# Row maxima twelve slots ahead of the scores in place of sixteen, with shifts in two equal halves, in a fused two-layer kernel

## The chip, the cores and the metric

The kernel runs as one program on one core of a Trainium2 chip. Its time is the device time of an execution in microseconds; the median of three runs before the change is 3403.16 us (3401.01 to 3411.55). TensorE does matrix products, VectorE and ScalarE work on tiles, GpSimd on a few more and on indirect transfers, and SyncE (SP) issues most of the transfers, in the order of its queue.

## The reference

Two layers over x of 16 batches x 512 positions x 128 features. Each layer normalises x and adds an "attention" and a "feed forward" part to it.

- Layer 0, first part: a small memory network is trained over chunks of the sequence and then read with queries made from every position.
- Layer 0, second part: a convolution over three positions, an attention of 16 heads of 8 features, layer normalisation, and eight experts of which all are computed and weighted by a softmax gate, then normalisation again.
- Layer 1, first part: a causal attention, a convolution of its result which gives new queries, a second causal attention with the same keys and values, and an output product.
- Layer 1, second part: 32 experts of which each position takes 8; every expert has a capacity of 128 rows.

```python
scores = jnp.einsum('bhqd,bhkd->bhqk', q, k) / jnp.sqrt(jnp.float32(dh))
attn = jax.nn.softmax(scores, axis=-1)
ctx = jnp.einsum('bhqk,bhkd->bhqd', attn, v)
...
ctx = _causal_attn(q, k, v)
...
q2 = conv_out.transpose(0, 2, 1).reshape(b, s, NUM_HEADS, HEAD_DIM)
ctx2 = _causal_attn(q2, k, v)
```

## The kernel before, in words

The program has four stages: the memory network's training (0 to about 353 us of the span), layer 0's attention (names with c_, to 1131), layer 0's experts (names with a_, to 2205), and layer 1 (names with b_, with the routed experts, r_, in between).

Both attentions use one class, `Attention`. A *turn* p is the attention of one batch: 16 in layer 0, 32 in layer 1, where each batch has a first and a second attention. In layer 1 the turns go: two firsts, then a first and a second by turns, then the last two seconds. A turn has 16 *slots* s, four *groups* g of heads with four tiles t of 128 positions each (s = 4 g + t). For a slot the kernel does three things, at different times:

1. maxima: TensorE makes the scores with the queries on the partitions (`tensor_maxima`, L1295, and the causal mask, L1301), and VectorE takes the maximum of each row (L1504). They go through a ring of two double banks, m.
2. scores: TensorE makes them again with the keys on the partitions (L1327, mask L1334), where the shift by the row maximum comes in as two extra rows of the queries' tile; ScalarE takes the exponential (L1445). They go through a ring of three banks, s.
3. values: the exponentials times the values, with the row sums (L1358). After two groups ScalarE copies the result out (`scalar_context`, L1452).

The shift rows must be in the queries' tile before the scores use them. When all maxima of some groups are there, TensorE transposes them (`tensor_shift`, L1308), VectorE negates and splits them into two bf16 rows (L1512, L1513), and SP sends them into the tile (`sync_shift`, L1273). Shift 0 covers three groups and is made in slot 12 of the turn before; shift 1 covers the fourth and is made in slot 0 of the turn itself, and is first used in slot 12.

The maxima of turn p + 1 are made in turn p, slot for slot: they run 16 slots ahead. So there is one turn at the start, p = -1, in which maxima run alone, and the last turn has scores alone.

The order is written out by hand for each engine, in loops over turns and slots; no scheduler moves anything. `extra` functions put further jobs into given slots: in layer 0 the convolution of batch p + 2 in slots 0 and 2 (L1761), its query projection in 4 (L1766), keys in 5 (L1769), values in 6 (L1776), and in the last turn the first batch of the next stage, by the table `FIRST`: z (the gate's and the memory's input), x1, gate, query, hidden, memory (L1787 to L1813). There VectorE makes the gate's probabilities in the query job, after an exponential on ScalarE, and GpSimd then does sixteen operations, two for each expert (L1742, L1743); VectorE's last work is the chain of the memory job, to L1927. The next stage starts with a barrier. In layer 1 the projections of a first attention are in slots 0, 4 and 8 (L2958, L2962, L2979), the convolution for a second in 7 and 9 (L2968), the normalising of a context in 6 (L1265), the output product in 10 (L2987), and the routed experts in turns 0 to 8 by the table in `Routed`: LOCAL, SELECT (the rows of four experts are found; five VectorE operations, L2725 to L2731), ROWS, UP (two products, L2645), GATE (VectorE, L2737, L2738), HIDDEN (transposes, L2651), DOWN (L2656 and scaling on ScalarE, L2702).

SP's queue in a turn of layer 1 is: store the spread sums and context of the former turn's second half, shift 1, the experts' weights, a read of the sum, the reciprocals' store and the reads of scale and context (`sync_inverse`: three waits), then the first half's spread, the twelve row transfers of turn p + 2 (`sync_rows`, each 16 partitions by 8 heads), and shift 0 of turn p + 1.

## Time and profile before

| | |
|---|---|
| median of three runs | 3403.16 us |
| the profiled execution | 3429.25 us, its span 3427.3 us |
| TensorE matmul busy | 3143.2 us, 92% of the span |
| VectorE, ScalarE, GpSimd busy | 2539.8 (74%), 2058.4 (60%), 851.4 (25%) us |
| granted TensorE clock, mean | 0.967 |
| layer 0's maxima on VectorE (L1504) | 512 x 1.212 us |
| layer 1's maxima on VectorE (L1504) | 768 x 1.041 us |

The page cuts the span in 40 slices and gives each engine's busy share in tenths; a matmul counts as busy while it is in the pipeline, so a full TensorE row means that it is never without work and not that it runs at its peak. A line of the timeline has the start in us, the time of the merged instructions in us, the engine, the line of the kernel, what is written from what, the shapes, the count, and in brackets the idle time before it and what ended that.

### The profile page before, as it was taken

The numbers are of one execution on the slowest core, as the hardware profiler recorded it, in microseconds if no ns is written. First come the engines' busy times: TensorE is split into PE (matmuls) and PEld (weight loads), VectorE is DVE, ScalarE is ACT, GpSimd is POOL, SyncE is SP. The second block draws the span as 40 slices with busy tenths as digits, with TensorE's granted clock in tenths as the row PEclk, the third lists the DMA queues.
The fourth block names the chain that finished last, engine by engine and source line by source line (L and its number), as shares of the span: only waits on it lengthen the run. The fifth ranks groups of instructions, "written<-read, shape, count | busy, mean of one in ns | idle before, by whom it ended". The sixth has DMA issues, their size and how long they took to land. (4 is left out here: it accounts for less than half of the span.)

```text
span 3427.3 us, 83140 instructions
## 1 busy us (share of the span) xinstructions
PE 3143.2 (92%) x33099; PEld 1864.5 (54%) x33099; DVE 2539.8 (74%) x5024; ACT 2058.4 (60%) x4153; POOL 851.4 (25%) x772
## 2 busy tenths in 40 slices
PE   6887599999999999999999999688999999999997
PEld 6876222222222677777777777545555555555553
DVE  5876788888887376677667667677777887777874
ACT  6774188888888444343443434146667766776775
POOL 3321111111111332332242233213333211111110
PEclk9998699999999999999999999789999999999998
DMA  4100222222221101011010001223333233222222
GB/s 144 32 13 1 57 74 83 83 80 81 77 71 61 37 28 31 22 33 35 22 33 29 29 23 33 54 75 89 87 87 79 85 94 86 76 82 82 80 64 62
DMA packets 234970, 204.86 MB, mean 60 GB/s; under 512 B 74340, under 2 KB 190852, under 8 KB 234500
## 3 DMA queue, kind: packets, MB, share of 16 engines
q1 hardware_dynamic: 227620, 194.71, 19.7%
q0 software_dynamic: 6144, 4.72, 1.0%
q8 instruction: 224, 3.67, 0.5%
q10 hardware_dynamic: 864, 0.79, 0.1%
q14 instruction: 118, 0.97, 0.1%
HBM read 73.61 MB, written 59.39 MB: 39 GB/s over the span
## 5 line engine op out<-in xcount | busy, mean ns | idle before, releaser
L1504 DVE TENSOR_REDUCE b_maxima<-psum 128x2 f32<-128x1024 f32 (+3 forms) x768 | 780.0, 1041 | 256.8 <-PE psum L1301 226.3
L1445 ACT ACTIVATE b_prob<-psum 128x512 f32<-128x512 f32 (+2 forms) x1536 | 725.8, 526 | 323.4 <-PE psum L1334 297.8
L1504 DVE TENSOR_REDUCE c_maxima<-psum 128x2 f32<-128x1024 f32 x512 | 592.2, 1212 | 60.4 <-PE psum L1295 59.6
L1445 ACT ACTIVATE c_prob<-psum 128x512 f32<-128x512 f32 x1024 | 547.4, 600 | 113.5 <-PE psum L1327 96.9
L2268 PEld LDWEIGHTS psum<-consts_layer,a_hid 128*128 128x128 f32 x4096 | 476.2, 192 | 53.6 <-issue 53.3
L2268 PE MATMUL psum<-consts_layer,a_hid 128*128 128x128 f32 x4096 | 477.8, 274 | 0.0
L2258 PE MATMUL psum<-a_x1t,consts_layer 128*128 128x512 f32 x1024 | 461.9, 595 | 14.1 <-ACT a_hid L2328 7.6
L2328 ACT ACTIVATE a_hid<-psum,consts_layer 128x512 f32<-128x512 f32 x512 | 347.1, 687 | 196.4 <-PE psum L2258 189.7
L1358 PE MATMUL psum<-b_prob,b_v 128*32 128x128 f32 (+3 forms) x5632 | 405.5, 374 | 15.1 <-ACT b_c L1452 14.0
L1327 PE MATMUL psum<-b_qa,b_ka 64*128 64x512 bf16 (+3 forms) x2048 | 349.0, 305 | 45.8 <-ACT b_prob L1445 30.4
L2495 DVE SCALAR_TENSOR_TENSOR a_acc<-psum,a_gprob,a_acc 128x128 f32<-128x128 f32 x512 | 143.7, 342 | 262.4 <-PE psum L2268 246.8
L1295 PE MATMUL psum<-b_ka,b_qa 62*128 62x512 bf16 (+3 forms) x2048 | 306.1, 306 | 28.6 <-DVE b_maxima L1504 17.3
L1358 PE MATMUL psum<-c_prob,c_v 128*32 128x256 f32 (+1 forms) x3840 | 320.2, 405 | 1.7 <-ACT c_prob L1445 0.6
L2258 PEld LDWEIGHTS psum<-a_x1t,consts_layer 128*128 128x128 f32 x1024 | 187.3, 191 | 217.1 <-issue 196.9
L1327 PEld LDWEIGHTS psum<-b_qa,b_ka 64*128 64x128 bf16 x2048 | 123.3, 94 | 304.3 <-ACT b_prob L1445 209.6
L1334 PE MATMUL psum<-b_kmask,b_pick 64*128 64x64 bf16 x4096 | 245.0, 191 | 0.5 <-issue 0.5
L1295 PE MATMUL psum<-c_ka,c_qa 62*128 62x512 bf16 x1024 | 209.9, 389 | 31.3 <-DVE c_maxima L1504 17.3
L1327 PE MATMUL psum<-c_qa,c_ka 64*128 64x512 bf16 x1024 | 218.3, 387 | 19.1 <-ACT c_prob L1445 18.7
L1301 PEld LDWEIGHTS psum<-b_qmask,b_pick 64*128 64x128 bf16 x4096 | 201.4, 97 | 53.6 <-issue 8.0
L1301 PE MATMUL psum<-b_qmask,b_pick 64*128 64x64 bf16 x4096 | 228.4, 191 | 1.6 <-issue 1.5
L1334 PEld LDWEIGHTS psum<-b_kmask,b_pick 64*128 64x128 bf16 x4096 | 187.1, 95 | 46.4 <-issue 4.2
L1358 PEld LDWEIGHTS psum<-c_prob,c_v 128*32 128x32 f32 x3840 | 75.6, 108 | 204.3 <-issue 111.6
(398 smaller groups left out, 4203.6 us busy)
## 6 DMA issues: line engine op xcount, KB each, us to landing
b_qa<-b_part SPq DMA_DIRECT2D x192, 128.0 KB
b_context<-b_c SPq DMA_DIRECT2D x64, 256.0 KB, 2.1
c_qa<-c_part SPq DMA_DIRECT2D x96, 128.0 KB, 2.5
b_ka<-b_part SPq DMA_DIRECT2D x96, 128.0 KB
c_ka<-c_part SPq DMA_DIRECT2D x90, 128.0 KB, 2.5
c_context<-c_c SPq DMA_DIRECT2D x32, 256.0 KB, 2.1
b_scale<-b_inverse SPq DMA_DIRECT2D x64, 128.0 KB
b_unscaled<-b_context SPq DMA_DIRECT2D x64, 128.0 KB
```

The lines of the kernel that those rows point to most:

```text
L1295: last = nc.tensor.matmul(out[:, half, k0:k0 + w], qa[rows, hh, t * P:(t + 1) * P], ka[rows, hh, 0:w], start=True, stop=not self.causal)
L1301: last = nc.tensor.matmul(out[:, half, k1:k1 + HALF], self.pick[n][rows, :], self.qmask[rows, :], start=False, stop=n == 1)
L1327: last = nc.tensor.matmul(outs[half][:, k0:k0 + w], ka[rows, hh, t * P:(t + 1) * P], qa[rows, hh, q0:S], start=True, stop=not self.causal)
L1334: last = nc.tensor.matmul(outs[half][:, k0 + n * HALF:k0 + (n + 1) * HALF], self.pick[n][rows, :], self.kmask[rows, :], start=False, stop= ...
L1358: product = nc.tensor.matmul(self.acc[32 * j:32 * (j + 1), q0:q1], self.values(p)[:, t, column:column + 32], self.prob[:, s % 2, j, q0:q1] ...
L1445: self.nc.scalar.activation(out, src, ACT.Exp, scale=SCALE).then_inc(self.s.free, 1)
L1504: self.nc.vector.reduce_max(out, src, X).then_inc(self.m.free, 1)
L2258: nc.tensor.matmul(bank[4 + u % 3], K("up0", e * F0 + f * P, P), x1t[n][:, :], start=True, stop=True).then_inc(up_ready.sem, 1)
L2268: last = nc.tensor.matmul(tiled(2 + e % 2)[:, t, :], hid[:, e % 2, f, t * P:(t + 1) * P], K("down0", (e * FC + f) * D, D), start=f == 0, s ...
L2328: nc.scalar.activation(hid[:, e % 2, f, :], bank[4 + u % 3], ACT.Relu, bias=K("upb0", u, 1)).then_inc(hid_ready.sem, 1)
L2495: last = nc.vector.scalar_tensor_tensor(acc[n][:, t, :], tiled(2 + e % 2)[:, t, :], gprob[n][:, t, e:e + 1], acc[n][:, t, :], ALU.mult, AL ...
```

## The change

- Maxima run 12 slots ahead (`LEAD`): in slot s of turn p the maxima of turn p + 1, slot s - 4, and in the first four slots those of turn p, slots 12 to 15 (`leading`).
- Shift 0 and shift 1 cover two groups each. Shift 0 stays in slot 12 of the turn before; shift 1 is made in slot 4 (before: slot 0) and first used in slot 8 (before: slot 12).
- SP sends shift 1 after `sync_inverse` of the former turn's second half, no longer before the weights.
- In layer 0's last turn the first batch's jobs stand in slots 4, 8, 9, 10, 11, 13 in place of 2, 6, 7, 8, 10, 13.
- The routed jobs: SELECT 5 for 4, UP 6 and 7 for 5 and 6, GATE 10 for 7, HIDDEN 11 for 9, DOWN 13 for 11.

```diff
--- before.py
+++ after.py
@@ -169,7 +169,8 @@
 BUFFERS = 3
 SPREAD = 16
 PAIRS = G // 2
-EARLY = G - 1
+EARLY = G // 2
+LEAD = SLOTS - T
 GAP = 16
 
 
@@ -1113,8 +1114,12 @@
 
     def moved(self, p, s):
 
-        jobs = [(p, 1)] if s == 0 else [(p + 1, 0)] if s == EARLY * T else []
+        jobs = [(p, 1)] if s == SLOTS - LEAD else [(p + 1, 0)] if s == EARLY * T + SLOTS - LEAD else []
         return [job for job in jobs if self.has(job[0])]
+
+    def leading(self, p, s):
+
+        return divmod(p * SLOTS + s + LEAD, SLOTS)
 
     def inverting(self, p, s):
 
@@ -1143,7 +1148,7 @@
                     for j in self.heads(s, 0):
                         self.s.add("exp", p, s, j)
                 jobs = [("shift", *job) for job in self.moved(p, s)] + more_m(p, s)
-                maxima = [("max", p + 1, s, u) for u in self.units(s)] if self.has(p + 1) else []
+                maxima = [("max", *self.leading(p, s), u) for u in self.units(s)] if self.has(self.leading(p, s)[0]) else []
                 for job in maxima[0:1] + jobs + maxima[1:]:
                     self.m.add(*job)
                 for job in more_s(p, s):
@@ -1369,8 +1374,9 @@
                     self.tensor_scores(pe, p, s, u)
 
             def maxima(u):
-                if self.has(p + 1) and u in self.units(s):
-                    self.tensor_maxima(pe, p + 1, s, u)
+                q, r = self.leading(p, s)
+                if self.has(q) and u in self.units(r):
+                    self.tensor_maxima(pe, q, r, u)
 
             def values(slots, half=None):
                 q, r = divmod(p * SLOTS + s - slots, SLOTS)
@@ -1491,10 +1497,8 @@
         if self.causal:
             t = T - 1 - t
         w = (t + 1) * P if self.causal else S
-        if g < EARLY:
-            out = self.maxima[0][:, :].rearrange("p (f g u t) -> p f g u t", f=2, g=EARLY, u=2)[:, :, g]
-        else:
-            out = self.maxima[1][:, :].rearrange("p (f u t) -> p f u t", f=2, u=2)
+        n, g = divmod(g, EARLY)
+        out = self.maxima[n][:, :].rearrange("p (f g u t) -> p f g u t", f=2, g=EARLY, u=2)[:, :, g]
         src = self.m.bank("max", p, s, u)
         if self.together(s):
             out, src = out[:, :, :, t], src[:, :, 0:2 * w].rearrange("p f (u k) -> p f u k", u=2)
@@ -1528,9 +1532,10 @@
 
     def vector_turn(self, dve, p, own, extra):
         for s in range(SLOTS):
-            units = self.units(s) if self.has(p + 1) else ()
+            q, r = self.leading(p, s)
+            units = self.units(r) if self.has(q) else ()
             for u in units[0:1]:
-                self.vector_maxima(dve, p + 1, s, u)
+                self.vector_maxima(dve, q, r, u)
             for job in self.moved(p, s):
                 self.vector_shift(dve, *job, own)
             for job in self.inverting(p, s):
@@ -1538,7 +1543,7 @@
                     self.vector_inverse(dve, *job)
             extra(p, s)
             for u in units[1:]:
-                self.vector_maxima(dve, p + 1, s, u)
+                self.vector_maxima(dve, q, r, u)
 
 
 @dataclass
@@ -1629,7 +1634,7 @@
         att.late(ctx, kept)
         CONVOLVE, QUERIES, KEYS, VALUES = (0, 2), 4, 5, 6
         LAST = NB - 1
-        FIRST = {2: "z", 6: "x1", 7: "gate", 8: "query", 10: "hidden", 13: "memory"}
+        FIRST = {4: "z", 8: "x1", 9: "gate", 10: "query", 11: "hidden", 13: "memory"}
 
         def job_of(p, s):
 
@@ -1677,8 +1682,6 @@
                 load_x(0)
                 load_x(1)
                 for p in range(-2, NB):
-                    if att.has(p):
-                        att.sync_shift(sp, p, 1)
                     if att.has(p - 1):
                         att.sync_spread(sp, p - 1, PAIRS - 1)
                     if att.has(p + 2):
@@ -1688,6 +1691,9 @@
                         load_x(p + 4)
                     if att.has(p - 1):
                         att.sync_inverse(sp, p - 1, PAIRS - 1)
+                    if att.has(p):
+                        att.sync_shift(sp, p, 1)
+                    if att.has(p - 1):
                         sp.wait_ge(att.normalised, p)
                         sp.dma_start(ctxt_d[(p - 1) * P:p * P, :], ctxt[:, :]).then_inc(ctxt_stored, 16)
                     if att.has(p):
@@ -2532,7 +2538,7 @@
 
 
 
-    LOCAL, SELECT, ROWS, UP, GATE, HIDDEN, DOWN = 2, 4, 1, (5, 6), 7, 9, 11
+    LOCAL, SELECT, ROWS, UP, GATE, HIDDEN, DOWN = 2, 5, 1, (6, 7), 10, 11, 13
     TOTAL, BEFORE, INCLUDED = 9, 10, 11
 
     def __init__(self, ctx, csem, nc, K, att, start, chosen, gate_up, down, table_d, sum_d):
@@ -2886,8 +2892,6 @@
                 for p in range(-1, len(turns) + 1):
                     if att.has(p - 1):
                         att.sync_spread(sp, p - 1, PAIRS - 1)
-                    if att.has(p):
-                        att.sync_shift(sp, p, 1)
                     routed.sync_weights(sp, p)
                     if p in outputs:
                         i, b = order.index(p), outputs[p].batch
@@ -2902,6 +2906,7 @@
                     if att.has(p - 1):
                         att.sync_inverse(sp, p - 1, PAIRS - 1)
                     if att.has(p):
+                        att.sync_shift(sp, p, 1)
                         att.sync_spread(sp, p, 0)
                     if att.has(p + 2):
                         att.sync_rows(sp, p + 2)
```

TensorE at the start of layer 0's attention, turn -1 and the end of the turn before: c_ka and c_qa are keys and queries (L1295, maxima), c_xt the convolution's input (L1761), c_xc its result (L1766 queries, L1769 keys, L1776 values). Before:

```order
L1776 MATMUL psum<-consts_layer,c_xc 128x128 x4
L1295 MATMUL psum<-c_ka,c_qa 128x512 x2
L1761 MATMUL psum<-c_xt,consts_layer 128x256 x3
L1295 MATMUL psum<-c_ka,c_qa 128x512 x8
L1761 MATMUL psum<-c_xt,consts_layer 128x256 x3
L1295 MATMUL psum<-c_ka,c_qa 128x512 x8
L1766 MATMUL psum<-c_xc,consts_layer 128x512
L1295 MATMUL psum<-c_ka,c_qa 128x512 x4
L1769 MATMUL psum<-c_xc,consts_layer 128x512
L1295 MATMUL psum<-c_ka,c_qa 128x512 x4
```

And in the changed kernel, whose lines are numbered up to six higher:

```order
L1782 MATMUL psum<-consts_layer,c_xc 128x128 x4
L1767 MATMUL psum<-c_xt,consts_layer 128x256 x6
L1300 MATMUL psum<-c_ka,c_qa 128x512 x2
L1772 MATMUL psum<-c_xc,consts_layer 128x512
L1300 MATMUL psum<-c_ka,c_qa 128x512 x4
L1775 MATMUL psum<-c_xc,consts_layer 128x512
L1300 MATMUL psum<-c_ka,c_qa 128x512 x4
L1782 MATMUL psum<-consts_layer,c_xc 128x128 x4
```

The two convolutions of slots 0 and 2 stand ahead of the first maxima now, and the query projection behind the first pair of them; eight pairs of maxima fewer stand ahead of the keys' projection.

SP in a turn of the middle of layer 1: b_spread and b_context are the stores of the row sums and the context, b_before a read of the sum, b_inverse, b_scale and b_unscaled the steps of `sync_inverse`, b_shift1 shift 1. Before:

```order
L1245 DMA b_spread1<-b_c1 128x1x32
L1246 DMA b_context<-b_c1 128x512
L1273 DMA b_qa0<-b_shift1 2x8x128 x2
L2900 DMA b_before<-sum 128x4x128
L1253 DMA b_inverse<-b_spread1 128x32
L1257 DMA b_scale<-b_inverse 64x1x512
L1260 DMA b_unscaled<-b_context 64x1x512
L1245 DMA b_spread0<-b_c0 128x1x32
L1246 DMA b_context<-b_c0 128x512
```

Changed:

```order
L1250 DMA b_spread1<-b_c1 128x1x32
L1251 DMA b_context<-b_c1 128x512
L2904 DMA b_before<-sum 128x4x128
L1258 DMA b_inverse<-b_spread1 128x32
L1262 DMA b_scale<-b_inverse 64x1x512
L1265 DMA b_unscaled<-b_context 64x1x512
L1278 DMA b_qa0<-b_shift1 2x16x128 x2
L1250 DMA b_spread0<-b_c0 128x1x32
L1251 DMA b_context<-b_c0 128x512
```

Shift 1 has moved from the third place to behind the context's read, with 16 head rows in place of 8.

VectorE in turn 2 of layer 1, from slot 4 on: r_tiles to r_index is the selection, b_cpad the normalising, r_th and r_h the gate, a row of b_maxima one reduction. Before:

```order
L1504 TENSOR_REDUCE b_maxima<-psum 128x2
L2725 TENSOR_SCALAR r_tiles<-psum 128x4
L2726 TENSOR_SCALAR r_below<-psum,consts_layer 128x512
L2729 TENSOR_REDUCE r_slot<-r_below 128x4
L2730 TENSOR_TENSOR r_slot<-r_tiles,r_slot 128x4
L2731 TENSOR_SCALAR r_index<-r_slot,consts_layer 128x4
L1504 TENSOR_REDUCE b_maxima<-psum 128x2 x3
L1504 TENSOR_REDUCE b_maxima<-psum 128x2x2
L1265 TENSOR_TENSOR b_cpad<-b_unscaled,b_scale 128x512
L1504 TENSOR_REDUCE b_maxima<-psum 128x2x2
L2737 SCALAR_TENSOR_TENSOR r_th<-r_th,r_gu 128x384
L2738 TENSOR_TENSOR r_h<-r_th,r_gu 128x384
```

Changed:

```order
L1508 TENSOR_REDUCE b_maxima<-psum 128x2
L1516 TENSOR_SCALAR b_shift<-psum 32x128
L1517 SCALAR_TENSOR_TENSOR b_shift<-psum,b_shift 32x128
L1508 TENSOR_REDUCE b_maxima<-psum 128x2 x2
L2731 TENSOR_SCALAR r_tiles<-psum 128x4
L2732 TENSOR_SCALAR r_below<-psum,consts_layer 128x512
L2735 TENSOR_REDUCE r_slot<-r_below 128x4
L2736 TENSOR_TENSOR r_slot<-r_tiles,r_slot 128x4
L2737 TENSOR_SCALAR r_index<-r_slot,consts_layer 128x4
L1508 TENSOR_REDUCE b_maxima<-psum 128x2
L1508 TENSOR_REDUCE b_maxima<-psum 128x2x2
L1270 TENSOR_TENSOR b_cpad<-b_unscaled,b_scale 128x512
```

The selection has moved behind the maxima of slot 4 and the first of slot 5, shift 1 stands ahead of it, and the gate is gone from here (it follows in slot 10).

## Rows read from the trace of the kernel before

**Rows 1.** Windows: stretch in us, busy us by engine with counts, clock, DMA, GB/s
```profile
391.00:421.00 30.00, 18.40 (x66) 4.59 (x64) 28.88 (x28) 2.12 (x4) 6.32 (x4) 0.62 0.20 55
478.00:1029.00 551.00, 533.22 (x4918) 158.10 (x4916) 486.74 (x485) 465.64 (x874) 98.30 (x65) 1.00 0.27 79
1029.00:1067.00 38.00, 36.27 (x366) 9.06 (x366) 37.36 (x39) 34.41 (x66) 1.27 (x1) 1.00 0.22 66
1124.00:1136.00 12.00, 5.58 (x23) 2.41 (x16) 5.82 (x12) 1.97 (x3) 3.18 (x5) 0.72 0.33 98
2205.00:2237.00 32.00, 24.19 (x236) 14.46 (x238) 23.59 (x27) 1.76 (x4) 13.03 (x19) 0.61 0.31 76
2650.00:3341.00 691.00, 644.06 (x11570) 355.83 (x11572) 549.91 (x641) 489.48 (x1041) 116.90 (x96) 1.00 0.29 81
3346.00:3378.00 32.00, 30.10 (x584) 16.45 (x576) 27.09 (x33) 23.63 (x51) 1.27 (x1) 1.00 0.16 50
3378.00:3410.00 32.00, 27.65 (x353) 12.06 (x349) 2.74 (x7) 22.17 (x48) 1.28 (x1) 0.84 0.22 66
```

**Rows 2.** Timeline, start of layer 0's attention, TensorE
```profile
378.07 0.61 PE L1295 MATMUL psum<-c_ka,c_qa 62*128 62x512 bf16 x2 [13.52 <-DMA c_ka<-c_part]
378.61 2.93 PE L1761 MATMUL psum<-c_xt,consts_layer 128*128 128x256 f32 x6
...
391.02 2.00 PE L1766 MATMUL psum<-c_xc,consts_layer 128*128 128x512 f32 x2
```

**Rows 3.** Timeline, last turn of layer 0's attention, all engines
```profile
1089.73 6.38 ACT L1445 ACTIVATE c_prob<-psum 128x512 f32<-128x512 f32 x12
...
1094.44 0.16 DVE L120 SCALAR_TENSOR_TENSOR c_tmp<-c_rstd 128x4 f32<-128x4 f32 x1
...
1101.59 0.66 PE L1804 MATMUL psum<-consts_shared,a_q 128*128 128x128 f32 x4
...
1106.95 1.05 POOL L1742 TENSOR_TENSOR c_share<-a_gprob,consts_layer 128x512 f32<-128x512 f32 x1 [0.19 <-DVE a_gprob L1910]
...
1115.98 2.05 PE L1813 MATMUL psum<-memw1t,c_ht 128*128 128x128 f32 x16
...
1121.00 1.12 DVE L120 SCALAR_TENSOR_TENSOR c_tmp<-c_rstd 128x4 f32<-128x4 f32 x1
...
1125.80 1.26 POOL L1743 TENSOR_TENSOR a_acc<-a_acc,c_share 128x512 f32<-128x512 f32 x1
...
1129.02 0.69 DVE L1927 TENSOR_TENSOR a_q<-a_q,c_rest 128x512 f32<-128x512 f32 x1
...
1131.28 9.07 PE L2258 MATMUL psum<-a_x1t,consts_layer 128*128 128x512 f32 x16 [6.42 <-PEq L1671]
```

**Rows 4.** Timeline, start of layer 1, TensorE
```profile
2205.26 0.61 PE L1295 MATMUL psum<-b_ka,b_qa 62*128 62x512 bf16 x2 [7.39 <-POOL b_cpad L2929]
...
2213.60 2.07 PE L2962 MATMUL psum<-b_xt,consts_layer 128*128 128x512 f32 x2
```

**Rows 5.** Timeline, shifts and scores in turns 0, 1 and 10 of layer 1
```profile
2281.07 1.13 SPq L1273 DMA_DIRECT2D b_qa<-b_shift  x2
...
2283.87 0.61 PE L1327 MATMUL psum<-b_qa,b_ka 64*128 64x512 bf16 x2 [4.56 <-DMA b_qa<-b_shift]
...
2667.74 0.60 SPq L1260 DMA_DIRECT2D b_unscaled<-b_context  x1
...
2672.59 0.39 PE L1327 MATMUL psum<-b_qa,b_ka 64*128 64x512 bf16 x2
```

**Rows 6.** Waits (us in all, times, longest) of 2237 to 2590 us; then timeline, turn 0
```profile
PE psum L1295 <- DVE b_maxima L1504: 9.7, 13, 2.9
PE psum L1327 <- DMA b_qa<-b_shift: 7.4, 2, 4.6
...
2251.88 2.04 DVE L2730 TENSOR_TENSOR r_slot<-r_tiles,r_slot 128x4 f32<-128x4 f32 x1
...
2256.21 0.34 PE L1295 MATMUL psum<-b_ka,b_qa 62*128 62x384 bf16 x2 [2.88 <-DVE b_maxima L1504]
```

## The prediction

> **What bounds the kernel now.** I read the summary and the slices of the page first: TensorE is busy for 92% of the span, and its slices fall at the start of each stage and at the very end. So I cut the span where both attentions start and stop [rows 1]. In the middle of layer 0's attention TensorE is busy for 533.2 of 551 us and VectorE for 486.7: TensorE decides. In the stretch from 1029 to 1067, which has no projections left, VectorE is busy for 37.4 of 38 us: without projections the maxima decide, two reductions of 1.21 us in a slot, 2.4 us. In the middle of layer 1 TensorE has 644 of 691 us. A change of order that moves no work off TensorE can win nothing there; it can only win where TensorE idles, and that is at the ends. At the first slots of layer 0's attention only maxima run, at half clock (0.62 granted), TensorE 18.4 of 30 us busy, VectorE 28.9. The start of layer 1 looks the same (0.61, 24.2 of 32). In the last turn of layer 1 the reader is to see that taking the maxima away saves nothing: 32 us with them, 32 without, with the granted clock falling from 1.00 to 0.84.
>
> **The start of layer 0's attention.** Now the maxima of slot 0 are the first to wait for the row transfers (13.52 us of idle TensorE), and the two convolutions of the next batch, in slots 0 and 2, stand behind them; so does the query projection of slot 4, at 391.02 [rows 2]. In the changed order both convolutions stand ahead of the first maxima, inside that wait of 13.5 us: the first takes 2.93 us, the second as much, and both are hidden. Right behind the first pair of maxima comes the query projection, at the place of the convolution that now starts at 378.61. So everything from that projection on comes 391.02 - 378.61 = 12.4 us earlier. Not all of it stays: between that point and the first score VectorE's maxima set the pace, but with the key and value projections at half clock TensorE takes part in it. The query projection took 2.00 us at half clock; those of keys and values, which ran partly at full clock, have as many columns. I charge 2.0 us (bounds: 0 if the clock rises as it does now, 3.0 if all three slots wait for TensorE). Term: -10.4.
>
> **The end of layer 0's attention.** The last turn gets four slots of maxima. A slot with them takes 2.4 us, one without 6.38/3 = 2.13 us, by twelve exponentials (three slots) in 6.38 us [rows 3]: 4 x 0.28 = 1.1 us. The first batch's jobs keep their number of matmuls. The router's chain is pushed more than the rest: its query job stands at slot 10 in place of 8, while the memory job stays at 13. GpSimd starts its sixteen operations when VectorE has made the gate's probabilities, and they last from 1106.95 to 1125.80 + 1.26 = 1127.06. VectorE ends its chain at 1129.02 + 0.69 = 1129.71, and the next stage begins at 1131.28, 1.57 us later. Two slots later less what the hidden job now does behind it (it moves from 10 to 11): from the query job at 1101.59 to the memory job at 1115.98 there are 14.4 us now; afterwards there are three slots (6.4), the query matmuls (0.66), the hidden ones (two products as wide as the query projection, at full clock: about 2) and about 0.5 of waits, 9.5. So the query job, and with it GpSimd's end, comes 4.9 + 1.1 = 6.0 us later, at 1133.1, and GpSimd takes VectorE's place as the one who ends last: 1133.1 - 1129.71 = +3.4. I take 3.3 (bounds: 1.1 if ScalarE gives the exponentials as much sooner as it idles there, 5 if the sixteen stretch). Nothing hides it: the next stage starts when all engines have ended. Half clock follows TensorE's idle time there now (0.72 granted and 5.6 us busy over 1124 to 1136, rows 1); with 3 us more of it I add 1.0 (0 to 3.4).
> GpSimd and VectorE disturb each other here: the same small operation L120 takes 0.16 us at 1094.44, without GpSimd, and 1.12 at 1121.00, beside it [rows 3]. The Trainium skill, page "SBUF — State Buffer", section "SBUF: two separate sides", has a rule for it: the two share a pair of ports under an exclusive lock, and a VectorE operation with two inputs in SBUF waits for a GpSimd operation that reads SBUF. By that rule the last additions of VectorE's chain (L1925, L1927), which are free of GpSimd today, would each wait up to 1 us, VectorE would end with GpSimd, and the sum would be about 1 us higher.
>
> **The start of layer 1.** The query projection (slot 0) no longer waits for maxima; it starts at 2205.3, takes 2.07, and the maxima of slot 4 with the key projection behind them start at 2207.3 and 2208.0. Now the latter starts at 2213.60 [rows 4]. Term: -5.6 (bounds -4 and -6.5). GpSimd clears the values buffers before it makes turn 1's parts and may start those later than the projection allows, but they are wanted four slots later than before.
>
> **The end of layer 1.** Four more slots have maxima, twelve have none. A turn costs 32 us either way [rows 1]. Term: +0.5 (-1 to +2).
>
> **Shift 1.** Its transpose, two VectorE operations and two transfers move from slot 0 to slot 4, with 32 rows in place of 16 (and 32 in place of 48 for shift 0; the widths read by TensorE and VectorE are 128 either way). TensorE must have it at slot 8, before at slot 12. On SP's queue it now stands behind the reciprocal's store, the scale and the context read. In a late turn of layer 1 the last of these is issued at 2667.74 and done issuing at 2668.34; the two shift issues take 1.13, to 2669.5. From the end of issue to the release of TensorE it took 1.67 us where it was waited for (2281.07 + 1.13 to 2283.87): landing at 2671.1. Slot 8's scores start at 2672.59 [rows 5]: 1.4 us to spare. The last two turns of layer 1 have no projections and take 32 us in place of 35; slot 8 comes sooner there, and I expect a short wait in each, together +0.5 (0 to 3). In layer 0 a turn is 44 us long and the slack is larger. I found no wait for rows in the middle, so their later need wins nothing.
>
> **The eight routed turns.** Waits of TensorE here: 7.4 us in 2 for shift 0, which the change leaves at slot 12 and behind the same twelve row transfers, and 9.7 us in 13 for VectorE's maxima, most of it behind the selection [rows 6]. In turns that prepare a first attention the selection is stretched by GpSimd's parts (2.04 us for an operation on 128x4 elements) and TensorE then idles for up to 2.9 us. At slot 5 it still lies within those parts (they run 6.5 us from slot 4's key projection), so the wait moves with it; then come normalising at slot 6 and, before, the gate at slot 7. The gate's 1.1 us leave this crowded stretch and shift 1's 0.56 enter it: -0.5 in four turns, -2. But the gate at slot 10 is followed by its transposes at slot 11, not two slots later. From the end of slot 10's maxima TensorE has values, scores and maxima of slot 11 to do, 1.6 us; VectorE needs 1.23 for the maxima and 1.11 for the gate, 2.4 with the start: TensorE waits 0.8, in the turns with an output product (1.1 us more for TensorE, 0.7 for VectorE) 0.4. Eight turns: +4.8. Term: +2.8, bounds -6 (the waits behind the selection vanish) and +9 (a whole microsecond more in each). I take the reckoned one, near the middle.
>
> **Sum.** -10.4 + 3.3 + 1.0 - 5.6 + 0.5 + 0.5 + 2.8 = -7.9 us. The profiled execution took 3429.25 us (span 3427.3, 1.95 around it), 0.8% over the median of 3403.16; the terms are waits and engine times that both executions have. 3429.25 - 7.9 = 3421.3 for a profiled one, 3403.16 - 7.9 = 3395.3 for the median.
>
> **Rivals.**
> A. The routed turns gain and layer 0's end costs only the maxima: -10.4 + 1.1 - 5.6 - 2 + 0.5 = -16.4, 3387. For it: ScalarE, which gives GpSimd's chain its exponentials, is not full in a slot without maxima; TensorE's longest waits for VectorE sit at the place that is thinned. Against it: GpSimd's chain is 20 us of its own work.
> B. The start is won and spent again: the maxima-only stretch is a full half-clock stretch already, and the waits in turns 0 to 8 for transfers and GpSimd (shift 0's 4.56 us in turn 0, rows 5) fall where they fell. With 3 us lost at layer 0's start, 5 at its end and 6 in the routed turns the sum is -12.4 + 3 + 5 + 1.0 - 5.6 + 0.5 + 0.5 + 6 = -2: 3401. Against it: the worst ends must come together.
> C. Slower: shift 1 lands after slot 8 begins, in every turn of layer 1. The point is 1.4 us of slack in rows 5; the reciprocal waits for a spread's landing and two round trips to memory lie between. If the queue is 2.4 us later than reckoned, 31 turns lose 1.0 us each: -7.9 + 31 = +23, 3426. For it: shift 0, with an equal lead, is waited for in two routed turns and in some late ones; against it: shift 0 stands behind twelve row transfers, shift 1 behind three.
>
> **How the numbers follow.** This kernel's timing can tell about 0.3%, 10 us, from no change: faster is below 3393, slower above 3413. The forecast (3395, own range 3389 to 3401) has 0.55, A 0.18, B 0.14, C 0.10, the rest 0.03. Faster: 0.4 of the forecast, all of A, a little of B: 0.42. Slower: C and most of the rest, with some for a new wait that I did not see: 0.13. Same: 0.45. The range takes A in at one side and B with half of the way to C's threshold at the other: 3383 to 3410.
>
> **What would show it.** The convolutions L1767 before 378 in the idle wait, and layer 0's first score at about 409 in place of 419.6; GpSimd's last operation before the next stage, ending after VectorE's; layer 1's first maxima right behind a projection; the turns in the middle of both attentions as long as before; no wait of L1332 for b_shift at slot 8 over 0.5 us; TensorE waiting for r_h before L2657. Wrong if layer 0's first score comes later than 412, or if the steady turns change their length by more than 0.2 us: then 46 turns outweigh both ends.

## The result, and the profile after

| | us |
|---|---|
| kernel before, median of 18 runs | 3400.86 (3395.38 to 3411.55) |
| changed kernel, median of 18 runs | 3395.92 (3392.42 to 3401.26) |
| ratio, 95% interval | 0.9986 (0.9979 to 0.9992) |
| second series of the changed kernel | 3397.07 against 3399.95, 0.9984 (0.9974 to 0.9995) |
| profiled execution of the changed kernel | 3401.26, span 3399.2 |

The gain is 0.14%, 4.9 us, inside "no change" as the prediction bounds it, though it is clear of zero. The time forecast, 3395.3, is met; the movement forecast, -7.9, is 3 us too large.

The two profiles shown first can't be subtracted: 3427.3 and 3399.2 us of span are 28 us apart where the medians are 5 apart. The kernel before took about 3400 us in three of the four series and 3426.95 (17 runs) in one, which ran on another chip than the two behind it; the profile ahead of the prediction is like that one's, the changed kernel's like the others'. A third profile of the kernel before, from a series in which it took 3400 (3398.55 us, span 3396.6), is what I compare with. Both kernels are cut at the same places: first maxima, first score and last turn of layer 0, the mixture's first and last product, first score of layer 1, its turn 9, its turn 31, the end. Columns as in [rows 1]; the kernel before first:

```profile
380.60:420.90 40.30, 24.98 (x89) 8.23 (x91) 35.88 (x34) 2.32 (x4) 6.32 (x4) 0.67 0.19 53
420.90:1079.20 658.30, 636.57 (x5872) 187.59 (x5868) 584.89 (x585) 556.48 (x1045) 105.87 (x70) 1.00 0.26 77
1079.20:1132.40 53.20, 43.03 (x385) 16.73 (x382) 26.15 (x76) 36.42 (x71) 23.43 (x21) 0.96 0.14 44
1132.40:2180.90 1048.50, 1040.71 (x6204) 776.38 (x6205) 700.12 (x2630) 422.11 (x649) 335.52 (x301) 1.00 0.10 31
2180.90:2237.70 56.80, 28.44 (x263) 18.01 (x263) 38.14 (x92) 2.66 (x6) 15.11 (x21) 0.61 0.23 59
2237.70:2598.80 361.10, 334.28 (x5486) 193.22 (x5484) 286.83 (x367) 252.54 (x555) 132.76 (x136) 0.97 0.37 89
2598.80:3350.90 752.10, 702.03 (x12707) 388.74 (x12704) 601.06 (x703) 536.59 (x1142) 125.58 (x105) 1.00 0.28 80
3350.90:3396.60 45.70, 27.35 (x397) 13.61 (x393) 4.55 (x10) 24.05 (x52) 2.54 (x2) 0.87 0.24 71
```

And the changed kernel (its second profile, 3393.32 us):

```profile
377.90:407.10 29.20, 17.61 (x63) 4.46 (x63) 26.82 (x26) 1.37 (x2) 6.32 (x4) 0.62 0.22 61
407.10:1065.80 658.70, 636.99 (x5874) 188.08 (x5872) 584.73 (x585) 556.36 (x1045) 105.85 (x70) 1.00 0.26 77
1065.80:1121.80 56.00, 43.51 (x402) 16.64 (x398) 39.50 (x85) 36.60 (x71) 23.98 (x21) 0.94 0.13 42
1121.80:2170.70 1048.90, 1041.31 (x6204) 776.79 (x6205) 700.06 (x2630) 421.86 (x649) 335.34 (x301) 1.00 0.10 31
2170.70:2222.00 51.30, 24.73 (x215) 15.88 (x215) 32.12 (x86) 2.66 (x6) 14.99 (x21) 0.60 0.28 68
2222.00:2591.00 369.00, 334.19 (x5486) 193.95 (x5483) 286.79 (x367) 252.41 (x555) 129.94 (x134) 0.97 0.36 87
2591.00:3345.10 754.10, 703.45 (x12710) 389.76 (x12708) 604.93 (x703) 536.54 (x1142) 126.25 (x107) 1.00 0.28 79
3345.10:3391.40 46.30, 28.64 (x445) 14.91 (x441) 10.59 (x16) 24.00 (x51) 2.54 (x2) 0.86 0.24 70
```

In the sixth row TensorE is busy for as long in both kernels, 334 us, and the stretch is 7.9 us longer: pure waiting. One execution of a stretch varies by a few us, so each is averaged over two or three profiles that have it unchanged (for the routed turns only from series in which the kernel before took 3400 us):

| stretch | before | changed | difference | predicted |
|---|---|---|---|---|
| start of layer 0 | 41.5, 42.1, 40.3 | 29.9, 29.2, 29.9 | -11.6 | -10.4 |
| turns 0 to 14 | 658.5, 658.7, 658.3 | 658.4, 658.7, 658.2 | 0 | 0 |
| last turn, to the next stage | 53.2, 53.2, 53.2 | 57.5, 56.0, 57.6 | +3.8 | +4.3 |
| mixture of experts | 1048.9, 1048.7, 1048.5 | 1049.7, 1048.9, 1049.4 | +0.6 | 0 |
| start of layer 1 | 56.9, 57.1, 56.8 | 51.4, 51.3, 51.4 | -5.6 | -5.6 |
| turns 0 to 8, routed | 361.1, 358.1 | 368.4, 369.0, 365.3 | +8.0 | +2.8 |
| turns 9 to 30 | 756.2, 752.8, 752.2 | 756.2, 754.1, 754.4 | +1.2 | +0.5 |
| last turn and end | 49.3, 45.5, 45.7 | 47.2, 46.3, 45.8 | -0.4 | +0.5 |

The sum is -4.0, the medians' difference -4.9; the part ahead of the first maxima, 378 to 381 us in all six profiles, is not in the table. (358.1 is a kernel whose layer 1 is the kernel before's, 365.3 one whose layer 1 is the changed kernel's; both are below.) The last two rows are within the spread: four more profiles with the changed kernel's turns 9 to 30 have 752.6 to 755.6 there, and 46.3 to 49.0 in the last turn and end.

The start of layer 0, TensorE, changed kernel, first profile; it answers to [rows 2]:

```profile
366.77 2.76 PE L1767 MATMUL psum<-c_xt,consts_layer 128*128 128x256 f32 x12
380.55 0.61 PE L1300 MATMUL psum<-c_ka,c_qa 62*128 62x512 bf16 x2 [11.02 <-DMA c_ka<-c_part]
381.08 2.07 PE L1772 MATMUL psum<-c_xc,consts_layer 128*128 128x512 f32 x2
```

The convolutions L1767 now stand ahead of the wait for the row transfers, inside it. The query projection follows the first maxima by 0.53 us; before it was 391.02 - 378.07 = 12.95 [rows 2]: 12.4 us sooner, as reckoned. The start of layer 1 answers to [rows 4]; the query projection stands ahead of the first maxima, the key projection right behind them:

```profile
2201.04 2.07 PE L2963 MATMUL psum<-b_xt,consts_layer 128*128 128x512 f32 x2 [7.25 <-POOL b_cpad L2934]
2203.05 0.61 PE L1300 MATMUL psum<-b_ka,b_qa 62*128 62x512 bf16 x2
...
2203.69 2.08 PE L2967 MATMUL psum<-b_xt,consts_layer 128*128 128x512 f32 x2
```

The last turn of layer 0, all engines, answers to [rows 3]; the next stage begins at 1126.33, in its last line:

```profile
1099.67 0.96 PE L1810 MATMUL psum<-consts_shared,a_q 128*128 128x128 f32 x4
...
1103.97 1.05 POOL L1748 TENSOR_TENSOR c_share<-a_gprob,consts_layer 128x512 f32<-128x512 f32 x1 [12.74 <-DVE a_gprob L1916]
...
1120.44 4.16 DVE L1929 SCALAR_TENSOR_TENSOR c_qk<-c_qk,c_rstd,mem 128x128 f32<-128x128 f32 x4
...
1122.93 1.26 POOL L1749 TENSOR_TENSOR a_acc<-a_acc,c_share 128x512 f32<-128x512 f32 x1
...
1125.36 0.69 DVE L1933 TENSOR_TENSOR a_q<-a_q,c_rest 128x512 f32<-128x512 f32 x1
1126.33 0.23 POOL L2349 MEMSET a_zeros<- 128x160 f32 x1 [2.14 <-POOLq L1676]
```

GpSimd ends at 1124.19 and VectorE at 1126.05: VectorE is the last. Its four scalings L1929 take 4.16 us beside GpSimd; the same four took 1.14 us before, behind GpSimd's end (at 1127.12, L1923).

Before, VectorE was not the last, though the prediction reads it so: it ended at 1129.71, and SyncE, which clears the stage's 64 semaphores behind its last two stores, at 1130.8. SyncE's row of these clears, first and last start in us, kernel before, changed kernel and the run exp_early below:

```profile
L75 SPq EVENT_SEMAPHORE_RANGE_CLEAR  x64: 25/30/49, 1126.7 to 1130.8; - x64
L75 SPq EVENT_SEMAPHORE_RANGE_CLEAR  x64: 25/30/49, 1120.4 to 1124.4; - x64
L75 SPq EVENT_SEMAPHORE_RANGE_CLEAR  x64: 25/30/49, 1118.0 to 1122.1; - x64
```

The routed turns, changed kernel: TensorE's waits from 2227.4 to 2595.8 (us in all, times, longest), which answer to [rows 6], and the new wait in turn 7:

```profile
PE psum L1300 <- DVE b_maxima L1508: 8.2, 8, 2.5
PE psum L2657 <- DVE r_h L2744: 6.7, 5, 1.4
...
PE psum L1332 <- DMA b_qa<-b_shift: 6.0, 2, 4.9
...
PE psum L2657 <- ACT b_prob L1451: 1.9, 3, 0.6
```
```profile
2546.71 0.82 DVE L2743 SCALAR_TENSOR_TENSOR r_th<-r_th,r_gu 128x384 f32<-128x384 f32 x1
2547.57 0.56 DVE L2744 TENSOR_TENSOR r_h<-r_th,r_gu 128x384 f32<-128x384 f32 x1
...
2548.27 0.61 PE L2657 MATMUL psum<-consts_shared,r_h 128*96 128x128 f32 x4 [1.39 <-DVE r_h L2744]
```

The transposes of the gate's values wait in all eight turns, 6.7 + 1.9 = 8.6 us. Before they never did.

Shift 1 in turn 10 of layer 1, which answers to [rows 5]: issued until 2642.1, scores of slot 8 at 2645.9, no wait.

```profile
2640.98 1.13 SPq L1278 DMA_DIRECT2D b_qa<-b_shift  x2
...
2645.91 0.39 PE L1332 MATMUL psum<-b_qa,b_ka 64*128 64x512 bf16 x2
```

### The profile page after: what moved, and what is told of

Same layout as the page of the kernel before. It is cut to its first block and busy times, and to the rows that moved or that the text cites. A ratio compares the mean times of both kernels' runs of the same rounds, so it can differ in the third digit from the quotient of the medians.

```text
span 3399.2 us, 83140 instructions
## 1 busy us (share of the span) xinstructions
PE 3119.3 (92%) x33099; PEld 1853.6 (55%) x33099; DVE 2545.7 (75%) x5024; ACT 2058.5 (61%) x4153; POOL 851.1 (25%) x772
## 5 line engine op out<-in xcount | busy, mean ns | idle before, releaser
L1508 DVE TENSOR_REDUCE c_maxima<-psum 128x2 f32<-128x1024 f32 x512 | 592.5, 1212 | 65.3 <-PE psum L1300 64.4
L2274 PEld LDWEIGHTS psum<-consts_layer,a_hid 128*128 128x128 f32 x4096 | 476.2, 192 | 53.6 <-issue 53.3
L1300 PE MATMUL psum<-c_ka,c_qa 62*128 62x512 bf16 x1024 | 209.2, 387 | 25.7 <-DVE c_maxima L1508 14.1
L1339 PEld LDWEIGHTS psum<-b_kmask,b_pick 64*128 64x128 bf16 x4096 | 185.8, 95 | 45.7 <-issue 3.1
```

What stands on the lines that cost most here:

```text
L1300: last = nc.tensor.matmul(out[:, half, k0:k0 + w], qa[rows, hh, t * P:(t + 1) * P], ka[rows, hh, 0:w], start=True, stop=not self.causal)
L1339: last = nc.tensor.matmul(outs[half][:, k0 + n * HALF:k0 + (n + 1) * HALF], self.pick[n][rows, :], self.kmask[rows, :], start=False, stop= ...
L1508: self.nc.vector.reduce_max(out, src, X).then_inc(self.m.free, 1)
L2274: last = nc.tensor.matmul(tiled(2 + e % 2)[:, t, :], hid[:, e % 2, f, t * P:(t + 1) * P], K("down0", (e * FC + f) * D, D), start=f == 0, s ...
```

## The experiments

All were timed beside the kernel before, whose median was 3426.95 in the first series (before_again, halves16, lead_l0, slots_back), 3399.95 in the second (halves16_oldsp, after_again, gate9, exp_early) and 3400.21 in the third (before_third, l0_only, best, best_first). In names: the "routed slots" are those of the selection, up, gate, hidden and down products. The diffs are cut to the lines that matter; a plus or minus is against the kernel that the text names, the changed kernel where it names none.

**The kernel before, profiled again.** No edit.

> The kernel before, unchanged, profiled a second time. Its first profiled execution took 3429.25 us, the median of 18 is 3400.9. Theory: that execution had more half clock than most in the eight routed turns, so the second one takes 3401 +- 6 us, and the stretch from the first score of turn 0 of layer 1 to that of turn 9, 384.7 us in the first, is 363 to 370 us. Rival: the first profile is typical there, the stretch is 385 us again, and the new slots of the routed work are what shortened it to 368.4 us in the changed kernel.

3423.05 us, routed turns 381.7. The theory failed, and the rival's 385 nearly came, but not for the rival's reason: in this series all 17 runs of the kernel before took 3421 us or more. What follows is that the first profile was no odd execution, and that a profile must be compared with one from a series in which the same kernel takes the same time.

> The kernel before, unchanged, once more. Both profiles of it that there are come from where it takes 3421 to 3429 us. Theory: where it takes 3400 the routed turns (first score of turn 0 to that of turn 9 of layer 1) take 357 us (355 to 360), 26 us less, and all other stretches the same; so the changed kernel's 368.7 there are 11 to 12 us more, which is what the ends win less what is measured. Rival: the routed turns take 368 us there too, and the missing gain went elsewhere.

3398.55 us, routed turns 361.1 (expected 355 to 360, rival 368), all other stretches as in the first two profiles within a few us. The theory holds nearly: 21 to 24 us of the difference between the profiles lie in the routed turns, and on equal ground the changed kernel spends 8 us more there, not 11 to 12.

**The halves alone, lead of 16.** SP's new order stays; the first batch and the routed work have their old slots. Against the kernel before:
```diff
-EARLY = G - 1
+EARLY = G // 2
+LEAD = SLOTS
```


> Only the equal halves of the shifts and SP's new order: the maxima keep their lead of 16, and the first batch and the routed work their slots. Shift 0 is made at slot 8 and needed at slot 16. Theory: the two waits of TensorE for shift 0 in the routed turns (4.56 and 2.80 us before) vanish, nothing else moves: 4 us faster than before (0 to 7). Rival: the halves are the change's main gain: 8 us or more. Rival: shift 1 with twice the rows is late at slot 4 somewhere: slower than before by 3 us or more.

3463.26, ratio 1.0105 (1.0090 to 1.0119): 36 us slower, the last rival's direction and far more than any of the expectations. The two waits for shift 0 that were to vanish are still there (4.9 and 0.3 us here, 5.1 and 2.2 in the next run, at the start of turns 1 and 3), though its maxima are ready four slots sooner. In layer 0's last turn, all engines, shift 1 is made at slot 0, but in the new order of SP's queue it stands behind the reciprocal of slot 3 and TensorE waits 3 us for it:

```profile
1101.77 1.13 SPq L1278 DMA_DIRECT2D c_qa<-c_shift  x2
1104.81 0.40 PE L1332 MATMUL psum<-c_qa,c_ka 64*128 64x512 bf16 x2 [3.00 <-DMA c_qa<-c_shift]
```

**The same with SP's queue in its old order.** Against halves16, layer 0's loop; the same is done in layer 1's, and the later place is taken out in both:
```diff
+                    if att.has(p):
+                        att.sync_shift(sp, p, 1)
                     if att.has(p - 1):
                         att.sync_spread(sp, p - 1, PAIRS - 1)
```


> The kernel before with the shifts in equal halves alone: lead 16, and SP's queue in its old order, shift 1 ahead of the spread, the inverse and the scale. Theory: halves16 loses 36 us for two reasons, the shift jobs of slot 8 beside the values there, about 32 us in layer 1, and SP's order, 3 us in layer 0's last turn (the wait for shift 1 at its slot 8); so this one loses 30 to 33 us to the kernel before. Rival: SP's order is what costs (shift 1 behind the inverse of slot 3): this one is within 5 us of the kernel before.

3424.17, 1.0066 (1.0053 to 1.0079): 22.5 us slower by the ratio, 24.2 by the medians, where 30 to 33 were expected and 5 by the rival; layer 0's end is back at 53.3. Both of the theory's causes are there. How much each costs is not shown: halves16 lost 36 us in a series in which the kernel before took 3427, this one 22.5 in one with 3400. The waits of TensorE in layer 1 (2240 to 3410) show the larger cause:

```profile
PE psum L2977 <- DVE b_maxima L1502: 15.2, 14, 1.9
...
PE psum L1308 <- DVE b_maxima L1502: 12.6, 10, 1.9
```

The shift's transpose (L1308) waits for maxima 12.6 us, and is not among the waits of the kernel before (third profile), while the values projection (L2977) waits 15.2 (10.1 before). All of these waits are in slot 8: with a lead of 16 the equal halves put a shift job there, beside the values projection. A lead of 12 puts it on slots 4 and 12. So the halves cost with the long lead; what they are worth with the short one was not tried apart from it.

**The lead of 12 in layer 0 alone, halves in both.** The routed work has its old slots:
```diff
+    def lead(self):
+        return SLOTS if self.causal else LEAD
```


> As halves16, with the lead of 12 and the new slots of the first batch in layer 0 alone. Theory: layer 0's start gives 11.6 us (first maxima to first score 29.9 in place of 41.5 us), its end takes 4.3 (last turn's first score to the next stage 57.5 in place of 53.2): 7 us faster than halves16. Rival: the stage behind gives the start back through the clock: no faster than halves16.

3453.28, 1.0075 (1.0062 to 1.0088): 10 us faster than halves16 (7 expected). Layer 0's start 29.9 and its end 57.7 us, as in the changed kernel; halves16's end had been 57.2 through the queue, so the end cost only 0.5 on top here.

**The routed slots as before, all else changed.**
```diff
-    ... GATE, HIDDEN, DOWN = 2, 5, 1, (6, 7), 10, 11, 13
+    ... GATE, HIDDEN, DOWN = 2, 4, 1, (5, 6), 7, 9, 11
```


> The changed kernel with the routed work at its old slots (selection 4, up 5 and 6, gate 7, hidden 9, down 11). Against lead_l0 it has the lead of 12 in layer 1 too. Theory: layer 1's start gives 7.4 us and its last turn 2; the wait of TensorE for the gate's values before their transposes (8.6 us over eight turns in the changed kernel) is gone, while the waits behind the selection come back, some 5: so it is 3 us faster than the changed kernel, 3393 us. Rival: the new slots pay, because the shift at slot 4 and the selection now crowd VectorE: 3 us or more slower than the changed kernel, 3399 us or more.

3423.67 against 3426.95, 0.9987 (0.9978 to 0.9995): the changed kernel's ratio. The interval is 3 us wide to either side, so neither the 3 us better nor the 3 us worse is ruled out; nothing speaks for either. The wait for r_h is gone, and another is there; TensorE's waits over the whole span:

```profile
PE psum L2673 <- DVE b_maxima L1508: 6.8, 8, 1.4
```

L2673 is the selection's product at slot 4, next to shift 1's transpose. It waited 1.0 us in all in the third profile of before. So leaving slot 4 takes a wait of 6.8 us away, and as the routed work was moved it pays 8.6 for it.

**The changed kernel again.**

> The changed kernel, unchanged, profiled a second time and timed beside the kernel before. Theory: the ratio is 0.9986 again; on a chip where the kernel before takes 3427 us the routed turns (first score of turn 0 to that of turn 9 of layer 1) take 388 to 394 us, against 381.8 of the kernel before there, so these turns give back some 8 us of what both starts win; on one where it takes 3401 they take 368 again. Rival: the routed turns take 368 us on either chip, and the new slots are worth 20 us.

0.9984 and 369.0 us in the routed turns, in a series with 3399.95 for the kernel before, as the theory has it. Its half on a chip where that takes 3427 us stays untested.

**The gate at slot 9.**
```diff
-    ... GATE, HIDDEN, DOWN = 2, 5, 1, (6, 7), 10, 11, 13
+    ... GATE, HIDDEN, DOWN = 2, 5, 1, (6, 7), 9, 11, 13
```


> The gate at slot 9 in place of 10, its transposes still at 11. Theory (the prediction's): the 8.6 us in which TensorE waits for the gate's values in front of their transposes, in eight turns, go to under 1; nothing takes their place, as VectorE has 0.7 us to spare in slot 9: 5 us faster than the changed kernel (3 to 8). Rival: slot 9 stands right behind the normalising of the values at slot 8, where VectorE is late already; the wait moves to the maxima of slot 9: within 2 us of the changed kernel.

3391.71, 0.9970 (0.9958 to 0.9981), 5.4 us under the changed kernel in the same series; its seven runs (3385.57 to 3393.17) all lie below the twelve of the changed kernel (3393.32 to 3401.24). The routed turns take 358.7 us here and 362.8 and 363.4 in the two other profiles with this gate (best, best_first, below). In turn 7, VectorE and TensorE, the values are ready 2.4 us ahead of the transposes:

```profile
2532.81 1.01 DVE L2744 TENSOR_TENSOR r_h<-r_th,r_gu 128x384 f32<-128x384 f32 x1
...
2536.26 0.64 PE L2657 MATMUL psum<-consts_shared,r_h 128*96 128x128 f32 x4
```

So the wait between gate and transposes is most of what the routed turns lost: 361.6 us on the mean of the three profiles, 6.0 under the changed kernel, still 2.0 over the kernel before. What the 2.0 are is open; they are no more than such profiles differ by.

**The router's exponential one slot sooner.**
```diff
-                    if job == "query":
+                    if job == "gate":
                         act.wait_ge(a.gsm_ready.sem, 1)
```


> The exponential of the router's values goes to ScalarE one slot sooner, behind the gate job in place of the query job. Theory: it is ready to run at 28 us of layer 0's last turn and runs at 34; one slot sooner GpSimd's sixteen operations begin 2 us sooner (33 us of the turn in place of 35.1) and fall off VectorE's last operations by as much: the next stage begins at 56 us of the turn in place of 57.5, 1.5 us faster than the changed kernel in the trace, too little for the timing. Rival: VectorE's chain behind the memory job sets the end by itself; nothing changes (57.5).

0.9984 (0.9975 to 0.9993): no change in the time, as expected. All engines, last turn of layer 0 (it starts at 1066.53):

```profile
1097.54 0.23 ACT L1838 ACTIVATE c_pexp<-c_gsm 128x32 f32<-128x32 f32 x1
...
1099.70 1.05 POOL L1748 TENSOR_TENSOR c_share<-a_gprob,consts_layer 128x512 f32<-128x512 f32 x1 [10.80 <-DVE a_gprob L1916]
...
1118.51 2.22 DVE L1929 SCALAR_TENSOR_TENSOR c_qk<-c_qk,c_rstd,mem 128x128 f32<-128x128 f32 x4
...
1121.49 0.69 DVE L1933 TENSOR_TENSOR a_q<-a_q,c_rest 128x512 f32<-128x512 f32 x1
1122.54 0.23 POOL L2349 MEMSET a_zeros<- 128x160 f32 x1 [2.74 <-POOLq L1676]
```

GpSimd starts 33.2 us into the turn (35.1 before the edit), the scalings take 2.22 us in place of 4.16, and the next stage begins at 56.0 in place of 57.5 (four other profiles with the exponential where it was have 57.6 or 57.7, best below, with it sooner, 56.2). The second profile of the changed kernel has 56.0 as well, as its query job ran 1.2 us sooner; it lacks the 3.4 us at half clock that the others have there. VectorE's chain (1122.18) and SyncE's clears (1122.1) now end together, so a still earlier GpSimd would win nothing more. And part of the 1.5 us is lost again behind the barrier: over the mixture's first 10 us the granted clock is 0.69 (0.76 in the changed kernel's first profile), and the stage takes 1050.3 us (1048.9 to 1049.7).

**The change in layer 0 alone.** Lead and halves as attributes of an attention; routed slots and SP's order in layer 1 as before.
```diff
+        self.lead, self.early = (SLOTS, G - 1) if causal else (LEAD, EARLY)
```


> The change in layer 0 alone (lead of 12, halves, new slots of the first batch, SP's new order there); layer 1's attention and the routed work are the kernel before's, instruction for instruction. Theory: layer 1's part of the change wins 6 at its start and loses 11 in the routed turns, so without it the kernel is 3 to 5 us faster than the changed one: 8 us under before, ratio 0.9977. Rival: what is lost is lost in layer 0's end and behind it, layer 1's part is a gain of 3 us or more: ratio above 0.999.

3390.31, 0.9974 (0.9962 to 0.9986), where 0.9977 was expected: half of the change seems to move more than all of it (0.9984 and 0.9986), though the intervals overlap and the times alone don't settle it. The stretches agree: routed turns 358.1, so 9.5 us less than in the changed kernel, against 5.5 us of layer 1's start that are not won.

**Both edits together.** The diffs of gate9 and exp_early.

> The changed kernel with the gate at slot 9 and the router's exponential one slot sooner. Theory: both gains add, 5.4 and 1.5 us: 7 us under the changed kernel, ratio 0.9965 against before. Rival: they do not add, ratio 0.9975.

3389.17, 0.9971 (0.9961 to 0.9982). With gate9's 0.9970 beside it the rival "they don't add" can't be told from the theory: the second gain is too small. With gate9 it is the fastest that was run, 0.3% under the kernel before and about 0.13% under the changed one; l0_only (0.9974) lies within the intervals of both.

**The first batch at its old slots on top.**
```diff
-        FIRST = {4: "z", 8: "x1", 9: "gate", 10: "query", 11: "hidden", 13: "memory"}
+        FIRST = {2: "z", 6: "x1", 7: "gate", 8: "query", 10: "hidden", 13: "memory"}
```


> As best, with the first batch's jobs at their old slots (2, 6, 7, 8, 10, 13) in spite of the maxima in slots 0 to 3. Theory (the prediction's): the last turn is longer mainly because the query job comes two slots later and takes GpSimd's chain and VectorE's with it; at the old slots only the maxima's 1.1 us are left: the next stage begins 53.5 us (52.5 to 54.5) after the last turn's first score in place of 56. Rival: the maxima of slots 0 to 3 hold VectorE when the first job's normalising stands behind them, and everything behind it comes as late as now: 56 us.

3396.71, 0.9988 (0.9979 to 0.9998): 7.5 us slower than best; the end takes 64.4 us (56.2 in best), worse than the rival said, so the theory failed. TensorE in slots 2 and 3 of the last turn:

```profile
1085.51 0.39 PE L1300 MATMUL psum<-c_ka,c_qa 62*128 62x512 bf16 x2 [4.21 <-DVE a_q L1891]
...
1091.44 0.61 PE L1300 MATMUL psum<-c_ka,c_qa 62*128 62x512 bf16 x2 [4.13 <-DVE c_maxima L1508]
```

The first job takes one of the two buffers that maxima and jobs share, and holds it until VectorE has normalised what is in it; the maxima of slots 2 and 3 queue behind that. These two waits, 8.3 us, are the whole difference; SyncE again ends last, 3.2 us behind VectorE. So the first job must not stand among the last maxima. Whether the others could keep their old slots was not tried.

## Why the prediction was right, and where not

- **Start of layer 0.** Right: -11.6 for -10.4. Of the 12.4 us only 0.8 were lost again, not the 2.0 charged for TensorE at half clock: the projections do take 2.07 us (granted clock 0.62), but most of it lies beside VectorE's maxima.
- **End of layer 0.** The size is right (+3.8 for +4.3; the 1.0 for half clock in that 4.3 is in part the mixture's +0.6), the path is not. GpSimd's start and its end came as worked out: the end 55.3 us into the turn, 55.0 reckoned. But the sum was built on VectorE as the one who ended last before, and "GpSimd takes VectorE's place" failed too. Before, SyncE ended last, and it follows the attention's last context copy on ScalarE, which ends 47.5 us into the turn, 5.7 us ahead of the next stage. In the changed kernel that copy ends at 50.3: 1.3 us later for the maxima (1.1 reckoned; it is what the second profile has), and 1.5 later because the granted clock is 0.50 from 1096.9 to 1100.3, which the second profile lacks. By this path alone the next stage would begin at 56.0. The rest is VectorE's: its chain was stretched by more than the idle time it had, 4.16 us for the four scalings in place of 1.14, and ended 1.9 us behind GpSimd. The rule of the Trainium skill named in the prediction ("SBUF — State Buffer", section "SBUF: two separate sides") foretold the direction: a VectorE operation with two inputs in SBUF waits for a GpSimd operation that reads SBUF. The trace agrees, but it was the scalings L1929 that paid, not the additions behind them (0.69 us each, as before); in exp_early, where GpSimd ends 2.0 us sooner, at 53.3 us of the turn, they take 2.22.
- **Start of layer 1.** Right (-5.6 for -5.6).
- **End of layer 1.** -0.4 for +0.5, inside its bounds, and within the spread. That a turn costs 32 us either way doesn't hold beyond the profile it was read from: from first to last score the last turn takes 32.3 us there, 28.6 and 28.5 in the second and third.
- **Shift 1.** Right: no wait at slot 8 in turns 9 to 31, 2.1 us to spare after 1.67 us of landing in the turn shown (1.4 reckoned). Rival C is refuted.
- **Routed turns.** This is the term that was mis-sized: +2.8 reckoned, +8.0 measured, inside the bounds (-6 to +9). The wait was put at 0.8 and 0.4 us, 4.8 in all, and is 1.4 and 0.6 to 1.1, 8.6 in all. The step that failed is "VectorE needs 1.23 for the maxima and 1.11 for the gate, 2.4 with the start", against TensorE's 1.6: at slot 10 the gate's two operations take 0.82 + 0.56 = 1.38, and from the start of the slot's last maxima at 2545.57 to the transposes there are 2.7 us, of which TensorE fills 1.3. The "-2" for the selection did not come either: the waits of TensorE at slot 5 behind VectorE were 9.0 us in the third profile of before and are 6.9 and 8.5, at slot 7. It moved with the work.
- **Sum.** With +8.0 in that term the prediction's own sum is -2.7; the other errors (-1.2, -0.5 and those of the other rows) bring it to -4.0, against -4.9 measured. That the time came out to 0.6 us is partly luck: the median of 18 runs of the kernel before is 2.3 us below the three-run median from which the 7.9 were taken.
- **Rivals.** A needed a gain in the routed turns; there was a loss. B had the place right ("won and spent again" in the routed turns, +6) but charged both ends too much.

The mixture's +0.6 us lies in its first products, at half clock: over its first 10 us the granted clock is 0.80, 0.85 and 0.85 in the three profiles of the kernel before and 0.76, 0.80 and 0.78 in the three with the changed layer 0, behind 7.9 us of idle TensorE in place of 6.4. The idle time alone doesn't decide it: exp_early has 0.69 behind 6.4 us.

Open: what brings the half clock of 1096.9 to 1100.3. TensorE waits 1.86 us shortly ahead of it, and in the second profile, without it, 1.84. The change in layer 0 alone with the earlier exponential was not tried.

## What to carry to other kernels

A shorter lead of a prologue stage wins what the fill of the pipeline costs, once for each start, and is paid in every turn in which the shifted jobs land beside others: 17 us were won at two starts and 12 given back, half of it by one product that followed its producer by one slot instead of two. When jobs are moved between slots, check for each pair of producer and consumer how many slots lie between them before and after, and which engine's queue fills them. Before a stage's end is forecast, look for the engine that ends last in the rows: here it was SyncE, clearing semaphores for 4.1 us, and not the compute engine with the longest chain. And subtract only profiles between which the same kernel takes the same time: here the first pair differs by 28 us for a change of 5.

## What the runs showed of the hardware

In one series, on chip 8, the kernel before took 3427 us with nothing else changed; on chips 4 and 11 it took 3400 (the first series' chip is not known). Five profiles are like the longer ones (the one ahead of the prediction too). Between the profiles of the kernel before, 21 to 24 us of the difference lie in the eight routed turns. All five have waits there whose releaser the profile does not know (it prints "remote"); none of the nine others has one. VectorE and ScalarE, second profile of the kernel before, 2220 to 2650 us:

```profile
DVE b_maxima L1504 <- remote: 19.9, 8, 3.7
...
ACT b_prob L1445 <- remote: 5.7, 3, 3.1
```

TensorE's gaps over 0.2 us sum to 37.3 us there and to 25.7 in the third profile, and its busy time is 342.5 us against 334.3, with nearly the same granted clock (0.96 and 0.97). What stalls the engines, and whether it is the chip, is open. The ratios of the changed kernel (0.9984, 0.9986) and of slots_back (0.9987) can't tell whether it matters for the change.
